# Keys' projection of the first attention: one fp32 product becomes three F32R products of split operands

## What is computed

```python
x = x + _L0_xattn_ref(_layernorm(x), ctx, ctx, Wq, Wk, Wv, Wo, mask)   # touched
x = x + _L0_ffn_ref(_layernorm(x), ...)
x = x + _L1_xattn_ref(_layernorm(x), ctx, ctx, ...)
x = x + _L1_ffn_ref(_layernorm(x), ...)

def _L0_xattn_ref(q, k, v, Wq, Wk, Wv, Wo, mask):   # 16 heads of 64
    Q, K, V = (q @ Wq), (k @ Wk), (v @ Wv)          # each into 16 heads; k = v = ctx
    Q, K = (rope(Q), rope(K))
    attn = einsum('bqhd,bkhd->bhqk', Q / 8, K)      # masked, then softmax
    return einsum('bhqk,bkhd->bqhd', softmax(attn), V) @ Wo
```

## Time and profile before

| what | value |
|---|---|
| median of 3 runs | 766.96 us (764.24 to 768.7) |
| profiled execution, own time | 766.92 us |
| its span | 765.1 us |
| mean granted TensorE clock | 0.984 of full speed |
| PE busy | 706.0 us, 92% of the span |
| PEld busy | 579.8 us, 76% |
| DVE busy | 570.7 us, 75% |
| ACT busy | 426.6 us, 56% |
| POOL busy | 368.8 us, 48% |

### The profile page before, as it was taken

One profiled execution on the slowest core, in us unless ns is written; L12 is line 12 of the kernel. 1 busy time (PEld: TensorE's weight loads), 2 busy tenths in 40 slices (PEclk: granted clock), 3 DMA queues, 4 the chain that ended last, 5 costly groups with the idle time before them and its releaser, 6 DMA issues.

```text
span 765.1 us, 24056 instructions
## 1 busy us (share of the span) xinstructions
PE 706.0 (92%) x9208; PEld 579.8 (76%) x9208; DVE 570.7 (75%) x1673; ACT 426.6 (56%) x911; POOL 368.8 (48%) x430
## 2 busy tenths in 40 slices
PE   3699999999999999999999999999999999986665
PEld 2478888888888888888888878888788788864333
DVE  4666876786787678678768666878778778868786
ACT  2334454544544455454544535656666676668897
POOL 2664564484466457447545724556554555510000
PEclk9789999999999999999999999999999999998999
DMA  9300000000000000000000000000000000000001
GB/s 263 98 10 10 2 11 11 10 0 8 8 0 8 8 8 0 8 8 0 8 0 0 2 10 10 6 11 7 6 8 4 8 4 4 1 2 15 29 28 42
DMA packets 23393, 12.99 MB, mean 17 GB/s; under 512 B 6272, under 2 KB 22480, under 8 KB 23344
## 3 DMA queue, kind: packets, MB, share of 16 engines
q1 hardware_dynamic: 22528, 11.96, 5.9%
q10 hardware_dynamic: 816, 0.36, 0.2%
HBM read 10.21 MB, written 2.10 MB: 16 GB/s over the span
## 4 chain that ended last, share of the span: by engine, by line
PE 81%; ACT 9%; DVE 4%; POOL 2%; issue 2%; ACTq 0%; DVEq 0%
PE bank L978 8%; PE bank L994 8%; PE bank L1014 7%; PE bank L1600 5%; PE bank L910 5%; PE bank L982 4%; PE bank L931 4%; PE bank L1005 3%; PE bank L912 3%; PE bank L911 3%; PE bank L1633 3%; ACT a_kr L1864 2%; PE bank L947 2%; PE bank L1618 2%; PE bank L1576 2%
## 5 line engine op out<-in xcount | busy, mean ns | idle before, releaser
L570 POOL TENSOR_TENSOR a_turned<-a_turned,a_rope 128x512 f32<-128x512 f32 x64 | 82.0, 1282 | 181.1 <-DVE a_turned L655 181.1
L829 ACT ACTIVATE a_probs<-bank 77x512 f32<-77x512 f32 x128 | 71.0, 592 | 66.3 <-PE bank L982 65.4
L807 ACT COPY a_vs<-bank 77x512 f32<-77x512 f32 x64 | 37.4, 584 | 102.4 <-PE bank L912 102.4
L652 DVE TENSOR_TENSOR a_straight<-bank,a_rope 128x512 f32<-128x512 f32 x64 | 44.1, 689 | 61.7 <-PE bank L912 57.3
L571 POOL TENSOR_TENSOR a_qr<-a_straight,a_turned 128x512 f32<-128x512 f32 x64 | 82.4, 1288 | 5.0
L978 PE MATMUL bank<-a_qr,a_kr 64*77 64x128 f32 x1024 | 71.0, 278 | 2.1 <-ACT a_probs L829 0.3
L978 PEld LDWEIGHTS bank<-a_qr,a_kr 64*77 64x77 f32 x1024 | 56.3, 145 | 16.9 <-ACT a_fold L824 9.0
L994 PE MATMUL bank<-a_vs,a_probs 77*64 77x65 f32 x2048 | 67.2, 223 | 0.8 <-DVE x_all L716 0.8
L994 PEld LDWEIGHTS bank<-a_vs,a_probs 77*64 77x64 f32 x2048 | 62.5, 137 | 5.0 <-DVE x_all L716 1.1
L1014 PE MATMUL bank<-a_wo,a_oTn 128*128 128x128 f32 x512 | 64.0, 278 | 0.0
L698 DVE TENSOR_REDUCE a_am<-bank 128x6 bf16<-128x462 f32 (+1 forms) x96 | 50.3, 581 | 17.5 <-PE bank L956 17.5
(11 more groups left out here) (258 smaller groups left out, 1903.9 us busy)
## 6 DMA issues: line engine op xcount, KB each, us to landing
out<-x_all SPq DMA_DIRECT2D x8, 256.0 KB, 2.3
x_all<-in_x_dram SPq DMA_DIRECT2D x7, 256.0 KB, 6.3
a_ctx_in<-in_ctx SPq DMA_DIRECT2D x16, 77.0 KB
a_mask_in<-in_mask SPq DMA_DIRECT2D x16, 77.0 KB
a_wv<-in_ctx SPq DMA_DIRECT2D x16, 77.0 KB
a_wq<-in_Wq SPq DMA_DIRECT2D x1, 512.0 KB, 5.2
a_wk<-in_Wk SPq DMA_DIRECT2D x1, 512.0 KB, 6.6
a_wv<-in_Wv SPq DMA_DIRECT2D x1, 512.0 KB, 7.5
```

Source lines behind the costliest of these rows:

```text
L570: steps.link(nc.gpsimd.tensor_tensor(tv, tv, rope[:, 1:2, :].broadcast_to([128, 4, S]), ALU.mult))
L652: steps.did(nc.vector.tensor_tensor(straight[k % 3][:].rearrange("p (n s) -> p n s", s=S), pv.rearrange("p (n s) -> p n s", s=S), rope[:, ...
L829: nc.scalar.activation(probs[:, 4 * g:4 * g + 4, :], ps[ST_BANK[g]][0:KL, :].rearrange("p (h s) -> p h s", s=S), ACT.Exp).then_inc(s_free[ ...
```

## The change

The split of `wk` is added (`wk_hi` by ACT, `wk_lo` by DVE) in slot 0, behind the exponentials on ACT and behind the normalisation on DVE. The keys of pair 0 stay as they were. From pair 1 on each keys product is three F32R products of `wk_hi`, `wk_lo` with the context's parts, and the group waits for `ctx_ready` too.

```diff
-    wq_hi, wq_lo, wv_hi, wv_lo = (sb(n, [128, 1024], F32R) for n in ("wq_hi", "wq_lo", "wv_hi", "wv_lo"))
+    wq_hi, wq_lo, wv_hi, wv_lo, wk_hi, wk_lo = (
+        sb(n, [128, 1024], F32R) for n in ("wq_hi", "wq_lo", "wv_hi", "wv_lo", "wk_hi", "wk_lo"))
...
                 normalise(b)
+                if first:
+                    dve.wait_ge(keys_split, 1)
+                    nc.vector.tensor_tensor(wk_lo[:], wk[:], wk_hi[:].bitcast(F32), ALU.subtract).then_inc(keys_split, 1)
                 if more:
                     rope_queries(p + 1, 1 - P, 3)
...
                 exps(b, (1, 2, 3))
+                if first:
+                    act.wait_ge(a_free[K_TASK[2][0]], a_count(0, K_TASK[2]) + 1)
+                    nc.scalar.copy(wk_hi[:], wk[:]).then_inc(keys_split, 1)
...
-        def project_keys(p, k):
+        def project_keys(p, P, k):
             T, (lo, hi) = K_TASK[k], K_GROUPS[k]
             bk = T[0]
             pe.wait_ge(a_free[bk], a_count(p, T))
+            if pair(p, 1):
+                pe.wait_ge(keys_split, 2)
+            if not pair(p, 0):
+                pe.wait_ge(ctx_ready, p + 1)
             for i in range(hi - lo):
-                last = nc.tensor.matmul(pa[bk][:, 2 * KL * i:2 * KL * i + 2 * KL],
-                                        wk[:, 128 * (lo + i):128 * (lo + i) + 128], ctxT[:], start=True, stop=True)
+                out, cols = pa[bk][:, 2 * KL * i:2 * KL * i + 2 * KL], slice(128 * (lo + i), 128 * (lo + i) + 128)
+                if pair(p, 0):
+                    last = nc.tensor.matmul(out, wk[:, cols], ctxT[:], start=True, stop=True)
+                else:
+                    last = split_product(out, wk_hi[:, cols], wk_lo[:, cols], ctxT_hi[P][:], ctxT_lo[P][:])
             last.then_inc(a_full[bk], 1)
```

More of the change, by code:

```diff
@@ L456, in layer0_attention @@
     roped, k_roped, cast_done, half_done = sem("roped"), sem("k_roped"), sem("cast_done"), sem("half_done")
-    weights_split, values_split, hi_ready, ctx_ready = (sem(n) for n in ("weights_split", "values_split", "hi_ready", "ctx_ready"))
+    weights_split, values_split, keys_split, hi_ready, ctx_ready = (
+        sem(n) for n in ("weights_split", "values_split", "keys_split", "hi_ready", "ctx_ready"))
     dve_step, pool_step = sem("dve_step"), sem("pool_step")
@@ L1026, in tensor @@
         for k in range(3):
-            project_keys(0, k)
+            project_keys(0, 0, k)
         project_values(0, 0, 1)
@@ L1067, in slot @@
                 if more:
-                    project_keys(p + 1, 0)
+                    project_keys(p + 1, 1 - P, 0)
                 turn_out(b - 1)
                 if more:
-                    project_keys(p + 1, 1)
+                    project_keys(p + 1, 1 - P, 1)
                 scores(b, P, j, 1)
                 if more:
-                    project_keys(p + 1, 2)
+                    project_keys(p + 1, 1 - P, 2)
                 if last_pair(p):
```

## The result

The changed kernel takes 775.95 us (median, 774.70 to 778.38) against 766.85 for the kernel before in the same runs: ratio 1.0131, 95% interval 1.0108 to 1.0154, so 9.1 us slower. The profiled execution took 776.46, with a span of 774.6.

The account below looks back on a forecast made before the run. PE was taken to bound the kernel, with F32R weight loads setting the keys' record distance: 767.0 + 15 x 0.65 (9.7) = 776.7 us, other edits at nothing. Likeliest case's range 775.5 to 782; overall range 760 to 788.

Parts of the forecast that it names:

- PE sets the time, one to one: First attention's loop: PE waits only 0.8 us in 380, so keys cost on PE changes the time equally, fifteen times.
- s = 0.1145: Distance in us between F32R keys records: 24 per pair make 2.75 us against 2.10, +0.65 per pair.
- my two nearest rows: Profile rows bounding the record distance: output projection's fp32 records at 0.111 us and queries' F32R records at 0.118.
- 128 of them are about 0.103: Loading 128 F32R weight columns at 0.80 ns each takes about 0.103 us, a floor for the keys' record distance.
- The entry costs the same and drops out: Going from bf16 records into a keys group costs PE about 0.05 us extra, both before and after the change.
- Nothing queued behind the keys gets a new wait either.: Behind the keys on PE, each group ends later only by its own growth; no cost was added.
- The sum: Keys' products in pairs 1 to 15: +0.65 us per pair, times 15, gives +9.7 us on 767.0.
- 0.6 to 0.7 was to be seen: Sign in the profile after: the pair's period on PE grows by 0.6 to 0.7 us.
- Split and added waits cost nothing: ACT's cast and DVE's subtraction fit in holes; ctx_ready waits taken as free, with 1.3 and 2.7 us kept for the range.
- The streaming rival: The stream sets the keys' record distance at 0.071 us: 6.0 us faster, 761.0 us; chance 0.12.
- the pass rivals: Narrow F32R keys products take more passes: 0.262 us each gives 830 us, chance 0.14; 0.136 gives 784.5, chance 0.06.
- Taken up elsewhere: PE's existing waits in the pair absorb the longer keys: no change, 767 to 770 us; chance 0.06.

Follow-up runs that it names:

- experiment 1: The changed kernel with the keys of all pairs left as fp32 products, split of wk and added waits kept: 766.61 us, ratio 1.0002 to the kernel before.
- experiment 11: The changed kernel without the wk_lo product and with DVE's normalised rows moved behind the last keys' rope and the residual: 762.80 us, ratio 0.9952 to the kernel before.
- experiment 2: The changed kernel with only 76 of the 154 context columns in the keys' products: 797.04 us (783.06 to 810.24), records 0.113 us apart.
- 5: The changed kernel with 120 of the 154 context columns in the keys' products: 776.82 us, ratio 1.0124 to the kernel before.
- 3: The changed kernel with 64 of the 128 weight columns in each keys product: 764.88 us, ratio 0.9981 to the kernel before.
- 6: The changed kernel with 96 of the 128 weight columns in each keys product: 764.28 us, ratio 0.9991 to the kernel before.
- run 9: The changed kernel with DVE's normalised rows moved behind the last keys' rope and the residual: 775.12 us, ratio 1.0100 to the kernel before.
- run 10: The kernel before with DVE's normalised rows moved behind the last keys' rope and the residual, as a control: 765.92 us, ratio 0.9991 to the kernel before.
- experiment 4: The changed kernel with keys records dealt one by one between the scores' bf16 folds and between the transposes: 777.99 us, ratio 1.0152 to the kernel before.
- run 12: The changed kernel with keys group 1 dealt between the transposes and DVE's normalised rows moved behind the residual: 770.17 us, ratio 1.0050 to the kernel before.

## Why the prediction was right, and where it wasn't

The time (776.7 forecast, 775.95 measured), the range and the sign were right. Point by point:

- *PE sets the time, one to one.* Right for what was added (experiment 1 leaves nothing beside the products), but not for what is removed: below the length of before, POOL and DVE take over (experiment 11).
- *The price of a record.* I took s = 0.1145; it is 0.111, the lower of my two nearest rows, the output projection's. "128 of them are about 0.103" was the right mechanism: experiments 2, 5, 3 and 6 move the context columns without effect and the weight columns with the effect of the load. The queries' 0.118 is then their stream, at the values' price per column. At 0.111 the sum was +0.56 per pair; the products cost 0.52 (in run 9 a pair takes 27.59 us, in run 10 27.07). "The entry costs the same and drops out" missed the rest: the first keys record starts 0.45 behind the bf16 group in place of 0.48, twice, and other gaps around the groups changed by hundredths both ways.
- *"Nothing queued behind the keys gets a new wait either."* This step failed. It compared what lies on PE and left out DVE's queue: the later end of keys group 1 moved DVE's rows from just ahead of POOL's operation to just behind it, they became 0.62 us longer, and the residual behind them is late for PE by 0.25 to 0.3. It is worth 3.3 of the 8.7 us in the loop. The prediction had no term for it.
- *The sum.* 9.7 was forecast for the products alone, 13 x 0.65 = 8.4 of it between pairs 0 and 13. They cost 6.8 us there, and PE no longer has the 1.4 of waits that it had before in pairs 0 and 1. The new wait adds 3.3, which makes 8.7. In the loop a pair grew by 0.79, where 0.6 to 0.7 was to be seen. So that the size came out is in part luck: an overpriced term and a missed one nearly met.
- *Split and added waits cost nothing.* Right as far as the runs tell: 766.61.
- *The rivals.* The streaming rival is excluded: with 64 weight columns, where the stream does set the distance, it is 0.074, with 128 columns 0.111. So are the pass rivals, which wanted 0.136 or 0.262, and so is a price per column: 76, 120 and 154 columns have one distance. "Taken up elsewhere" held for the 1.4 us of pairs 0 and 1.

What stays open: why the runs with 76 columns and with only the transposes mixed had stops of over 4 us at the first record of a slot with 51 and 42 packets of instructions. The same interleaving with DVE's move (run 12) and the 120-column kernel did not have them in their profiled executions, so neither edit brings them by itself.

## What to carry to other kernels

Count a stream of different weights by the longer of this product's stream and the next one's load, pair by pair in queue order: three short F32R products in place of one fp32 product (two records here) are no saving when each brings a full fp32 load, 3 x 0.111 = 0.333 us against 0.262. Where TensorE's work grows by a few tenths in a slot, follow the event that comes later through the in-order queues of the other engines, and look for operations of DVE and POOL that now change their order; a wait shorter than a matmul record's length doesn't show in the list of waits, only as a longer group.

## What the runs showed of the hardware that I had not expected

- F32R weights load no faster than fp32 ones: 138, 165, 192 ns for 64, 96, 128 columns, 0.84 ns a column; 128 fp32 columns took 190.
- F32R streams at 0.46 ns a column at the full clock (0.118 for 256, 0.24 for 512), a little more than the 0.42 that one column per step of 2.4 GHz would be.
- Only one load is ahead: mixing wide-load and narrow-load products doesn't average their costs (experiment 4, 0.18 to 0.19 against 0.139). This is the rule that fits the folds; the transposes miss it by 0.02.
- Two DVE instructions of 128 columns each took 0.60, 1.46 or 2.08 us together, by where POOL's operations lay.
- A stop of TensorE of 4.5 us cost 8: behind it the granted clock was 0.50 (experiment 2).
